# Second projection of a two-layer transformer block: which engine scales and shifts the rows that are turned for the product

## What is computed

```python
x = x + _layernorm(_L0_attn_ref(_layernorm(x)))          # rows z, kept in `hold`
x = _layernorm(x)                                         # (z - mean) / std
h = _rmsnorm(x, ln1_w)                                    # x * rsqrt(mean(x*x) + eps) * w
qkv = jnp.einsum('bsh,oh->bso', h, wqkv)                  # 256 -> 384
q, k = rope(q), rope(k)                                   # then attention, experts
```

## Time and profile before

| | us |
|---|---|
| median of 3 runs | 2657.15 (2654.84 to 2660.06) |
| the profiled execution, its own time | 2659.51 |
| its span | 2657.1 |
| the loop of `project_two`, 1384.0 to 1480.3 | 96.3 |

### The profile page before, as it was taken

One profiled execution on the slowest core, in us unless ns is written; L12 is line 12 of the kernel. 1 busy time (PEld: TensorE's weight loads), 2 busy tenths in 40 slices (PEclk: granted clock), 3 DMA queues, 4 the chain that ended last, 5 costly groups with the idle time before them and its releaser, 6 DMA issues. The chain is left out here.

```text
span 2657.1 us, 46148 instructions
## 1 busy us (share of the span) xinstructions
PE 2305.0 (87%) x13138; PEld 1476.5 (56%) x13138; DVE 1727.0 (65%) x4529; ACT 1485.3 (56%) x3264; POOL 1039.7 (39%) x1795
## 2 busy tenths in 40 slices
PE   4899999999999999999837599999999857999990
PEld 3666666666666667666423233333333545888880
DVE  6777764777557774777269678777777375444445
ACT  3666664666556663666338477777777543333332
POOL 0355442555345543455406222222222104555554
PEclk8999999999999999999869699999999867999995
DMA  2011110011001110101124311111111441111115
GB/s 91 17 29 26 29 29 15 20 29 30 25 20 30 26 29 15 30 20 29 27 71 163 106 36 36 35 36 36 36 27 27 167 142 46 53 53 51 53 47 194
DMA packets 140998, 131.40 MB, mean 49 GB/s; under 512 B 74336, under 2 KB 110944, under 8 KB 139616
## 3 DMA queue, kind: packets, MB, share of 16 engines
q1 hardware_dynamic: 131552, 109.64, 14.0%
q0 software_dynamic: 9216, 18.96, 2.4%
HBM read 87.58 MB, written 33.88 MB: 46 GB/s over the span
## 5 line engine op out<-in xcount | busy, mean ns | idle before, releaser
L1275 ACT ACTIVATE b_P<-b_SC 128x512 f32<-128x512 f32 (+3 forms) x768 | 328.7, 499 | 163.4 <-PE b_SC L1378 162.0
L294 POOL TENSOR_TENSOR a_A<-a_A,a_P 128x512 f32<-128x512 f32 (+3 forms) x320 | 306.8, 959 | 279.3 <-PE a_O L633 268.5
L463 ACT ACTIVATE a_P<-a_SC 128x512 f32<-128x512 f32 (+3 forms) x640 | 292.2, 469 | 173.5 <-PE a_SC L616 166.7
L521 DVE CUSTOM_DVE_ANT_0 a_MX<-a_MX,a_causal 128x128 f32<-128x128 f32 (+3 forms) x512 | 248.5, 502 | 150.2 <-PE a_MX L689 144.6
L1217 POOL TENSOR_SCALAR_AFFINE_SELECT b_P<-b_P 128x128 f32<-128x128 f32 x512 | 146.1, 292 | 443.9 <-ACT b_P L1275 434.2
L333 POOL TENSOR_SCALAR_AFFINE_SELECT a_P<-a_P 128x128 f32<-128x128 f32 x448 | 169.6, 385 | 339.6 <-ACT a_P L463 334.6
L615 PE MATMUL a_SC<-a_QR,a_KR 128*128 128x512 f32 (+3 forms) x768 | 296.1, 389 | 5.6 <-DMA a_QS<-a_minusT 3.4
L1325 DVE CUSTOM_DVE_ANT_0 b_MX<-b_MX,b_causal 128x128 f32<-128x128 f32 (+3 forms) x512 | 248.9, 499 | 79.5 <-PE b_MX L1427 77.2
L689 PE MATMUL a_MX<-a_KR,a_QR 128*128 128x512 f32 (+3 forms) x768 | 270.3, 361 | 28.3 <-DVE a_peak L521 24.4
L1427 PE MATMUL b_MX<-b_K,b_Q 96*128 96x512 bf16 (+3 forms) x768 | 251.3, 339 | 42.4 <-DVE b_peak L1325 14.5
L616 PE MATMUL a_SC<-a_QS,a_KS 65*128 65x512 f32 (+3 forms) x768 | 265.3, 349 | 0.0
(11 more groups left out here) (277 smaller groups left out, 4626.0 us busy)
## 6 DMA issues: line engine op xcount, KB each, us to landing
a_inv<-inv_rows SPq DMA_DIRECT2D x128, 128.0 KB, 3.1
stack_rows<-p_stk SPq DMA_DIRECT2D x32, 480.0 KB, 2.6
a_W<-in_w_pair SPq DMA_DIRECT2D x34, 384.0 KB, 3.8
b_stk<-stack_rows SPq DMA_DIRECT2D x136, 96.0 KB, 2.1
W<-in_w SPq DMA_DIRECT2D x8, 1024.0 KB, 7.9
c_E<-done_rows SPq DMA_DIRECT2D x8, 1024.0 KB, 6.6
n_x<-in_x SPq DMA_DIRECT2D x4, 1024.0 KB, 9.3
a_fold<-a_total SPq DMA_DIRECT2D x256, 1.0 KB, 1.8
```

Of the source, the lines that this page charges most:

```text
L294: eng.tensor_tensor(acc[h][c][:, a:], acc[h][c][:, a:], buffer(n, h)[:, a:], ALU.add).then_inc(added[h], 1)
L463: act.activation(buffer(n, h)[:, a:], SC[h][:, a:], ACT.Exp, scale=DH1 ** -0.5).then_inc(s["exp_done"], 1)
L521: dve.tensor_tensor_reduce(MX[c % MAX_BANKS1][:, 0:w], MX[c % MAX_BANKS1][:, 0:w], causal[:, BANK - w:], 1.0, 3 * NEG, ALU.add, ALU.max, p ...
L1275: act.activation(probs[k % RING2][:, a:], SC[k % SCORE_BANKS][:, a:], ACT.Exp, scale=DH2 ** -0.5).then_inc(s["exp_done"], 1)
```

## The change

`narrow` moves from VectorE's list to ScalarE's. It stays two instructions for each step, with the same inputs and the same output, now `activation` with `Identity`, a scale and a bias. In ScalarE's step it stands between `values` and `feed`, and waits there for `turned` as it did on VectorE. The four instructions ahead of the loop move too, behind a new signal on `var_ready`, and in the last step none is made any more.

```diff
             link(dve.tensor_tensor(sm["hshift"], shift_z, sm["ratio"], ALU.mult))
+            dve.sem_inc(s["var_ready"], 1)
...
-            def narrow(r, p):
-                for u in range(2):
-                    t = r * 2 + u
-                    dve.tensor_scalar(HN[p][:, u, :], tile_of(rows, t, 0),
-                                      small["hscale"][:, bass.ds(t, 1)], small["hshift"][:, bass.ds(t, 1)],
-                                      ALU.mult, ALU.add).then_inc(s["hn_ready"], 1)
...
-                dve.wait_ge(s["turned"], r + 1)
-                narrow((r + 2) % NR, p)
-
-            for i in range(2):
-                narrow(i, i)
...
+            def narrow(r, p):
+                for u in range(2):
+                    t = r * 2 + u
+                    act.activation(HN[p][:, u, :], tile_of(rows, t, 0), ACT.Identity, scale=small["hscale"][:, bass.ds(t, 1)],
+                                   bias=small["hshift"][:, bass.ds(t, 1)]).then_inc(s["hn_ready"], 1)
...
                 if not last:
+                    act.wait_ge(s["turned"], r + 1)
+                    narrow((r + 2) % NR, p)
                     feed(r + 1, 1 - p)
...
+            act.wait_ge(s["var_ready"], 5)
+            for i in range(2):
+                narrow(i, i)
             feed(0, 0)
```

## The result

| | before | after |
|---|---|---|
| median, us | 2656.55 (4 runs) | 2681.05 (4 runs, 2677.17 to 2684.12) |
| ratio to before | | 1.0078, 95% interval 1.0062 to 1.0094 |
| profiled execution, its own time | 2659.51 | 2680.47 |
| its span | 2657.1 | 2678.4 |

The medians lie 24.5 us apart; the profiled execution took 2680.47, 21.0 more than that of before. The prediction was 2685, which is 28 more than before, with a range of 2665 to 2704. What follows explains the 21 us of the profiled execution.

The account below looks back on a forecast made before the run. VectorE was taken to bound the loop at 5.33 us a step. Fourteen steps of 5.92 with start and end gave +9.5 us, clock falls +18.6: +28, 2685 us, range 2665 to 2704.

Parts of the forecast that it names:

- VectorE set the pace before: In the loop before the change, VectorE was the fullest engine and its list set the step at 5.33 us.
- ScalarE's list, 5.49 us: ScalarE's own loop step: 4.64 us plus 0.98 for two activations, less 0.13 overlap, 5.49 at the least.
- The ring, 5.92 us: Loop cycle through ScalarE's `feed`, TensorE's product and ScalarE's `values`: from 4.47 to 5.92 us with `narrow` and queue instructions inside.
- the step of 4.55 us: Gap between two products before the change, at 1426.01 and 1430.56, read as the ScalarE-TensorE cycle setting the time.
- The falls of the clock, 18.6 us: Loop products slowed to 1.2 GHz by TensorE's longer idle time: 7 of 14 steps, 2.65 us each.
- Start and end: Loop edges: first activations some 0.5 us earlier, step 1's product at 1395.1 for 1394.88; the end 0.9 us shorter.
- The ring rules, the clock holds: Rival for the loop: only two or three clock falls, as before; +13 us, 2671; chance 0.25.
- No slower: Rival: queue instructions run ahead under ScalarE's work in the loop; +3.5 us, 2661, within 0.2%; chance 0.12.
- Faster: Rival: ScalarE's pauses swallow both activations and the loop step falls to 4.64 us; 2649; chance 0.03.

Follow-up runs that it names:

- the control: Kernel before, scaled rows kept on VectorE, with ScalarE's and VectorE's 16 steps written out so addresses are constants: 2656.51 us, ratio 0.9992.
- behind `feed`: Changed kernel with ScalarE's two scaled-row activations placed after `feed` in its step, no longer between `values` and `feed`: 2664.7 us, ratio 1.0017.
- both edits: Changed kernel with ScalarE's 16 steps written out and TensorE doing two more unread products a step: 2657.69 us, ratio 0.9996.
- the extra products: Changed kernel with TensorE doing two more products of 384 columns a step, into an unread bank, while it waits for `feed`: 2666.25 us, ratio 1.0024.
- the second execution: Changed kernel measured once more, unaltered, against the kernel before: 2676.67 us, ratio 1.0062.
- the doubled rows: Kernel before, VectorE's scaled rows kept, ScalarE making them again into an unread buffer at the changed kernel's place: 2678.37 us, ratio 1.0072.
- the split: Kernel before, but ScalarE scales the first tile of each pair behind `feed`, VectorE the second at its old place: 2658.4 us, ratio 0.9998.

## Why the prediction was right, step by step

**VectorE set the pace before.** Right as a reading: in the kernel before VectorE hardly waited for another engine in the loop (0.8 us in all from 1396 to 1468, the lines are in the last section). But the control shows that some 0.3 of its 5.33 us went with the loop kept: written out, it runs at 5.05 us a step with the same operations.

**ScalarE's list, 5.49 us.** Right for the bare list: 5.52 behind `feed`, 5.46 to 5.59 with both edits. But the prediction put the queue work into the ring only. It stands in ScalarE's list as well, and in the changed kernel that list comes to about 5.98.

**The ring, 5.92 us.** Right in sum: 5.98 in the timeline above, 83.0 us for 14 steps with the clock held against 82.9 predicted. That it ends last at full clock was not right: there ScalarE's list does, by some 0.06 us, as the missing wait ahead of `values` shows. The same holds for the step of 4.55 us that the prediction took for the ring at work: its rows show no wait ahead of the `values` of 1429.23 either. One price in the ring was off, too. I took 0.139 us for each queue instruction from `values`; those of `narrow` on ScalarE last 0.079:

```profile
L1016 ACTq FUSED_REGOPS  x91: 61/79/115, 1399.5 to 1488.7; - x91
L1016 ACT ACTIVATE p_hn<-hold,p_hshift,p_hscale x34: 584/600/601, 1385.0 to 1488.8; 128x256 f32 x28, 128x256 f32<-128x256 f32 x6
```

Four of them make 0.32 us, and yet it is 0.54 from `values` to `narrow` (I had 0.56); with the queue work gone it is 0.10. So a price too high made up for something that I had at nothing, and no run shows what: that this term came out is luck. Both activations took 1.06 (I had 0.99), and from the product's end to the second `values` it was 0.47 (I had 0.40), which is ScalarE's list ending later.

**The falls of the clock, 18.6 us.** The mechanism was right, shown by the extra products: with PE kept at work no fall is left. The number came out too, 7 of the 14 steps (8 in the second execution), but "half" was a choice between the bounds and not worked out, so its hit is partly luck. The term was too large. I had priced a slow step at 2.65 us more, as if the whole product ran at 1.2 GHz. The slow products took about 4.5 us and not 5.49, since full clock came back within each of them, and the steps 7.4 to 7.7 and not 8.57. The better price, 4.54 for 2.84, stood in the earlier trace rows already. The granted clock of the loop was 0.82 for the same reason, where I had said near 0.75. From product 1 to product 15 the changed kernel took 94.3 us (1395.92 to 1490.23); with the clock held 83.0. So the term measured 11.3 us.

**Start and end.** I expected the first activations 0.5 us before VectorE's old start; they begin at 1384.98, after it. But in this execution `hshift` too ended 0.9 us later than before (1384.89, read from the row at 1384.70), which the change doesn't touch. Behind `hshift` the first product starts 0.2 us earlier than before. In step 0 it is 0.98 from the start of `narrow` to that of `feed`, as said; the product of step 1 stands 1.04 after that of before, of which 0.9 is that delay. From the last product's start to the end of the loop it was 12.5 us and is 10.9 (1490.23 to 1501.11), 1.6 less, where I had 0.9.

The sum: 94.3 - 72.7 = 21.6 between the products, 1.0 at the start, -1.6 at the end: 21.0 us on the loop, where I had 28, and 0.9 of these 21.0 is the later `hshift`. Against the medians, 24.5 us apart, the forecast looks better than its sum deserves: of its terms the clock's was 7 us too large.

**The rivals.** "The ring rules, the clock holds" is what the extra products make of the kernel: 1.0024, with no fall at all. "No slower" would have needed queue work that runs ahead; the idle time before `narrow` excludes that here, and writing out ScalarE's list and holding the clock gave it. "Faster" fell with the doubled rows and with the split. Where VectorE is fullest in a loop, moving work to ScalarE, which the Trainium skill's page "Perfetto Trace Analysis" (Optimizing Scalar/DVE Operations) says may make sense, may still not pay: 1.0062 to 1.0078 here. Moving half of the rows behind `feed` gave 0.9998.

## What to carry to other kernels

Before moving an operation to the engine with room, draw the rings through it, not only its sum: an operation between what an engine takes from TensorE and what it gives back lengthens TensorE's ring by its whole length, its register work included. Put that register work into the engine's own list, too, and compare the two: here they came within 0.1 us of each other, and which ended last changed with TensorE's clock. Behind the hand-over the same operation cost about a quarter as much here. Where TensorE then waits longer in each turn, read the granted clock: idle time can be paid for twice.

## What the runs showed of the hardware

TensorE's waits cost clock here: half clock came in 7 and 8 of 14 steps, and with useless products in the wait in none, which gained 0.4 to 0.5% of the kernel's time (1.0024 against 1.0062 and 1.0078). The wait ahead of a single product does not tell whether that product is slow: with PE busy for 0.79 us ahead of the product at 1421.43 half clock followed, with 0.82 ahead of the one at 1415.45 it did not.

I had not expected what writing out a list does for VectorE. In the loop its two `tensor_scalar` took 0.755 us each at the median, and I had put that down to the operation beside GpSimd's work. In the control with constant addresses (line view, and the timeline of a step: L1093 the product, L884 `rotate`):

```profile
L963 DVE TENSOR_SCALAR p_hn<-hold,p_hscale,p_hshift x36: 396/407/962, 1382.7 to 1469.8; 128x256 f32<-128x256 f32 x36
```

```profile
1416.64 2.84 PE L1093 MATMUL p_QKV<-p_w,p_hT 128*128 128x384 f32 x8 [1.61 <-ACT p_hT L1027]
...
1417.31 1.83 POOL L884 TENSOR_TENSOR p_rot<-p_rot,p_crs 128x320 f32<-128x320 f32 x2 [1.02 <-DVE p_crs L980]
...
1418.01 1.27 DVE L963 TENSOR_SCALAR p_hn<-hold,p_hscale,p_hshift 128x256 f32<-128x256 f32 x2
...
1421.72 2.84 PE L1093 MATMUL p_QKV<-p_w,p_hT 128*128 128x384 f32 x8 [1.63 <-ACT p_hT L1027]
```

There the pair takes 1.27 us. Its instructions are short (0.40) and long (up to 0.96) by about halves, so the median of 0.407 says little of the pair. It ends at 1419.28, just behind GpSimd's second rotation (1419.14). In the loop kept a pair took 1.4 to 1.6 (1.42 and 1.63 in two steps). VectorE's waits from 1396 to 1468, first in the kernel before, then in the control:

```profile
DVE p_hn L963 <- issue: 2.3, 7, 0.4
DVE p_rot L978 <- issue: 1.5, 5, 0.4
DVE p_rot L988 <- ACT p_stk L1040: 0.8, 2, 0.5
...
DVE p_rot L988 <- ACT p_stk L1041: 5.5, 15, 1.3
```

The 3.8 us of "issue", some 0.28 a step, are gone with the loop, and 0.15 to 0.36 a pair came off `narrow`. VectorE did not keep all of it: it now waits for `first_part` 15 times, so at 5.05 us something else than its own list ends last. A ring through `first_part`, `rest`, `cross` and `rotate` is the likely one, but no run here tests it. How much of the shorter pairs is the form of the addresses and how much the order in which the two engines meet, no run separates either.
